# Delta layer: the filter table loaded in four parts around the rows, five buffers for the filter matrices, Gram copies in the room of the squares

## What is computed

```python
q = _short_conv(hidden_states @ Wq.T, conv_q)          # same for k and v; four taps, then silu
beta = jax.nn.sigmoid(hidden_states @ Wb.T)
delta_out = _delta_rule_chunkwise(q, k, v_direct, beta)
local_s = _fir(v_direct, fir_s)                        # 3, 15 and 63 taps, one filter per channel
local_m = _fir(v_direct, fir_m)
local_l = _fir(v_direct, fir_l)
o = probs[..., 0:1] * local_s + probs[..., 1:2] * local_m + probs[..., 2:3] * local_l \
    + probs[..., 3:4] * delta_out + probs[..., 4:5] * v_direct
```

## Time and profile before

| | |
|---|---|
| median of three runs | 4577.64 us |
| profiled execution | 4567.55 us |
| its span | 4565.8 us |
| busy: PE, DVE, ACT, POOL | 84%, 56%, 42%, 44% |

### The profile page before, as it was taken

The page is one execution under the profiler, slowest core; times in us unless marked ns, Lnnn a source line. Parts: engine busy times, 40 slices in busy tenths (PEclk is TensorE's granted clock), DMA queues, the critical chain, the costliest instruction groups (busy, mean ns, idle before and its releaser), DMA issues. The chain is left out here.

```text
span 4565.8 us, 70606 instructions
## 1 busy us (share of the span) xinstructions
PE 3829.3 (84%) x26088; PEld 2661.1 (58%) x26088; DVE 2545.7 (56%) x4540; ACT 1897.9 (42%) x3440; POOL 2020.5 (44%) x2061
## 2 busy tenths in 40 slices
PE   5677796799999519958999799788888888999995
PEld 2555774466767319943544455466666666656663
DVE  5566563455454582247777432498888887412223
ACT  3224132333333202225666412488888886112222
POOL 3531463323232216632332211298999998332223
PEclk8788897899999859978999999899999999999997
DMA  4774642200000529954544210111111111822224
GB/s 113 234 226 137 199 120 74 84 5 19 10 19 6 173 70 295 297 152 135 151 138 137 65 63 28 51 50 41 49 47 52 52 47 52 278 92 45 46 46 131
DMA packets 333687, 459.66 MB, mean 101 GB/s; under 512 B 70838, under 2 KB 245366, under 8 KB 329222
## 3 DMA queue, kind: packets, MB, share of 16 engines
q1 hardware_dynamic: 310710, 424.27, 30.5%
q0 software_dynamic: 22512, 30.36, 3.6%
q10 hardware_dynamic: 128, 0.52, 0.0%
HBM read 314.54 MB, written 140.51 MB: 100 GB/s over the span
## 5 line engine op out<-in xcount | busy, mean ns | idle before, releaser
L3565 POOL TENSOR_TENSOR mamba_hC<-mamba_h_t,mamba_cb 128x512 f32<-128x512 f32 x512 | 678.3, 1353 | 68.5 <-DVE mamba_h_t L3078 63.2
L3078 DVE TENSOR_TENSOR_SCAN mamba_h_t<-mamba_dA,mamba_pB 128x512 f32<-128x512 f32 x512 | 597.2, 1207 | 122.8 <-PE mamba_pB L3456 47.1
L3456 PE MATMUL mamba_pB<-ident,mamba_dBT 128*128 128x128 f32 x2048 | 328.8, 285 | 55.0 <-DVE mamba_h_t L3078 49.6
L3254 ACT ACTIVATE mamba_dA<-mamba_delta,mamba_a_neg 128x512 f32<-128x512 f32 x512 | 356.7, 713 | 21.5 <-DVE mamba_h_t L3078 20.9
L3456 PEld LDWEIGHTS mamba_pB<-ident,mamba_dBT 128*128 128x128 f32 x2048 | 240.4, 144 | 190.7 <-issue 99.0
L3465 PE MATMUL mamba_pY<-ident,mamba_hC 128*128 128x128 f32 x2048 | 321.3, 281 | 15.1 <-POOL mamba_hC L3565 14.1
L1911 POOL TENSOR_SCALAR mqa_prob<-mqa_prob,mqa_rinv 128x128 f32<-128x128 f32 (+3 forms) x256 | 136.7, 534 | 424.9 <-DVE mqa_rinv L1687 423.9
L2350 DVE TENSOR_REDUCE mha_nmax<-mha_pM 128x1 f32<-128x384 f32 (+3 forms) x352 | 215.9, 635 | 106.4 <-PE mha_pM L2658 103.2
L3245 ACT ACTIVATE mamba_dBT<-mamba_eT,mamba_b_t 128x512 f32<-128x512 f32 x384 | 273.8, 713 | 0.1
L1501 POOL DMA_INDIRECT top_sum<-top_y,top_xg x71 | 110.4, 1555 | 352.3 <-ACT top_y L1290 341.9
L3465 PEld LDWEIGHTS mamba_pY<-ident,mamba_hC 128*128 128x128 f32 x2048 | 248.1, 145 | 24.2 <-POOL mamba_hC L3565 23.5
(11 more groups left out here) (617 smaller groups left out, 8931.8 us busy)
## 6 DMA issues: line engine op xcount, KB each, us to landing
expert_w<-in_L_ffn_W SPq DMA_DIRECT2D x48, 1024.0 KB, 5.9
delta_shared<-delta_w SPq DMA_DIRECT2D x64, 576.0 KB, 4.9
mamba_cb<-mamba_c SPq DMA_DIRECT2D x128, 256.0 KB, 3.1
mha_qkT<-mha_parts_d SPq DMA_DIRECT2D x96, 256.0 KB, 5.1
delta_w<-delta_wst SPq DMA_DIRECT2D x32, 576.0 KB, 2.8
expert_w<-in_L_ffn_W SPq DMA_DIRECT2D x48, 256.0 KB, 6.4
top_w<-in_L_ffn_w SPq DMA_DIRECT2D x24, 512.0 KB, 10.7
top_slots<-top_y SPq DMA_DIRECT2D x1, 9159.0 KB, 36.5
```

The lines of the kernel that those rows point to most:

```text
L3078: nc.vector.tensor_tensor_scan(h_t[:, n % RH, :], dA[:, n % RA, :], pB[n % 2][:, :], 0.0, ALU.mult, ALU.add).then_inc(z["scan_ready"], 1)
L3254: nc.scalar.activation(dA[:, n % RA, :], delta[:, a % 2, ct, :], ACT.Exp, scale=a_neg[:, ct, s:s + 1])\
L3456: last = nc.tensor.transpose(pB[n % 2][:, tok(t)], dBT[:, r % RS, t, ct * P:(ct + 1) * P], c.ident[:, :])
L3565: nc.gpsimd.tensor_tensor(hC[:, n % RO, :], h_t[:, n % RH, :], cb[:, r % RC, :], ALU.mult)\
```

## The change

Five edits, all in `stage_delta`.

1. The table is loaded in four parts of 8 groups, sixteen transfers each (`load_table`): part 0 behind rows 1, part 1 behind rows 2, part 2 behind stores 0 to 3, part 3 behind rows 3, which now stand behind stores 4 to 7.
2. GpSimd has five buffers for filter matrices (`built_in`): the two of `wst` and three in `vn`, for matrices 0 to 24; the last seven use the two of `wst`. It builds matrices 0 to 2 in front of the deviation of rows 2 and 3 to 7 in front of that of rows 3.
3. 28 stores stand in front of the stores of V, the last four behind those of beta, in front of beta's load; none are left in the filter phase. The load of `vn` also waits for the stores out of it.
4. `gs` moves to `sq2`. VectorE's wait for the Gram stores moves from between its copies of K to the memset of the pads of `vp`, behind the gate copies.
5. V goes ahead of Gram copies 1 to 3, on TensorE, ScalarE and SyncE; V's load goes ahead of that of the Gram matrices.

```diff
+        spare = vn[:, :, :].rearrange("p a d -> p (a d)")[:, 0:3 * WCOLS].rearrange("p (n x) -> p n x", x=WCOLS)
+        built_in = [wst[:, 0, :], wst[:, 1, :], spare[:, 0, :], spare[:, 1, :], spare[:, 2, :]]
+        place = [g % 5 if g < 25 else (g - 25) % 2 for g in range(FG)]
+        turn_of = [place[:g].count(place[g]) for g in range(FG)]
...
-        gs = kr[:, NCH // 2:, :].rearrange("p n d -> p (n d)").rearrange("p (a t h i) -> p a t h i", a=NCH // 4, t=4, h=H)
+        gs = sq2[:, :, :, :].rearrange("p s k i -> p (s k i)").rearrange("p (a t h i) -> p a t h i", a=NCH // 4, t=4, h=H)
...
                 def store_table(g):
                     sp.wait_ge(z["w_built"], g + 1)
-                    sp.dma_start(w_d[g], wst[:, g % 2, :]).then_inc(w_st[g % 2], 16)
+                    sp.dma_start(w_d[g], built_in[place[g]]).then_inc(w_st[place[g]], 16)
+
+                def load_table(part):
+                    some = slice(part * FG // 4, (part + 1) * FG // 4)
+                    for r in range(R):
+                        sp.dma_start(table[C8 * r:C8 * (r + 1), some, :],
+                                     h_d.rearrange("(g c) x -> c g x", c=C8)[:, some, R - 1 - r:R - 1 - r + RUN])\
+                            .then_inc(table_in[part], 16)
...
@@ -4318,13 +4329,24 @@
                             sp.dma_start(h_d.rearrange("(k p) x -> p k x", p=P), hp).then_inc(z["h_st"], 16)
                             late_weights()
                             sp.wait_ge(z["h_st"], 16)
-                            for r in range(R):
-                                sp.dma_start(table[C8 * r:C8 * (r + 1), :, :],
-                                             h_d.rearrange("(g c) x -> c g x", c=C8)[:, :, R - 1 - r:R - 1 - r + RUN])\
-                                    .then_inc(z["table_in"], 16)
+                            load_table(0)
+                        if a == 2:
+                            load_table(1)
+                            for g in range(4):
+                                store_table(g)
+                            load_table(2)
+                            for g in range(4, 8):
+                                store_table(g)
+                        if a == 3:
+                            load_table(3)
                     if hf == 0:
-                        for g in range(3 * FG // 4):
+                        for g in range(8, FG - 4):
                             store_table(g)
+                    sp.wait_ge(z["vr_ready"], NCH // 2 * (hf + 1))
+                    for bb in range(HB):
+                        for i in range(CH // R):
+                            sp.dma_start(rows_of_runs(v_d, hf, bb, i, 0, NCH), vr[half_lanes(bb, i), :, :])\
+                                .then_inc(z["v_st"], 16)
                     for i in range(NCH // 4):
                         n = NCH // 4 * hf + i
                         sp.wait_ge(z["g_ready"], 2 * n + 2)
@@ -4332,11 +4354,13 @@
                             sp.dma_start(systems_by_row(g_d, hf, bb)[:, 4 * i * H:(4 * i + 4) * H, :],
                                          gs[lanes(bb), i, :, :, :].rearrange("p t h i -> p (t h) i"))\
                                 .then_inc(z["g_st"], 16)
-                    sp.wait_ge(z["vr_ready"], NCH // 2 * (hf + 1))
-                    for bb in range(HB):
-                        for i in range(CH // R):
-                            sp.dma_start(rows_of_runs(v_d, hf, bb, i, 0, NCH), vr[half_lanes(bb, i), :, :])\
-                                .then_inc(z["v_st"], 16)
+                    sp.wait_ge(z["v_st"], 16 * HB * CH // R * (hf + 1))
+                    if hf:
+                        sp.wait_ge(z["o_st"], 16 * hf)
+                    else:
+                        for i in range(2, 5):
+                            sp.wait_ge(w_st[i], 16 * place.count(i))
+                    sp.dma_start(vn[:, :, :], runs_of(v_d, hf)).then_inc(z["vn_in"], 16)
...
-                    sp.wait_ge(z["v_st"], 16 * HB * CH // R * (hf + 1))
-                    if hf:
-                        sp.wait_ge(z["o_st"], 16 * hf)
-                    sp.dma_start(vn[:, :, :], runs_of(v_d, hf)).then_inc(z["vn_in"], 16)
+                    if hf == 0:
+                        for g in range(FG - 4, FG):
+                            store_table(g)
...
                         if hf == 0:
-                            sp.wait_ge(w_st[g % 2], 16 * (g // 2 + 1))
+                            sp.wait_ge(w_st[place[g]], 16 * (turn_of[g] + 1))
                         if n >= 3:
                             sp.wait_ge(z["w_used"], n - 2)
                         sp.dma_start(wr[:, n % 3, :], w_d[g]).then_inc(w_ld[n % 3], 16)
-                        if hf == 0 and g < 4:
-                            store_table(3 * FG // 4 + 2 * g)
-                            store_table(3 * FG // 4 + 2 * g + 1)
...
                     dve.wait_ge(z["vr_ps"], NCH // 2 * (hf + 1))
                     nc.vector.memset(xt[:, :, :, :], 0.0)
-                    last = nc.vector.memset(vp[:, :, :, 0:PAD * HB], 0.0)
-                    last.then_inc(z["pads"], 1)
...
-                        if i == NCH // 4:
-                            dve.wait_ge(z["g_st"], 64 * NCH // 4 * (hf + 1))
                         nc.vector.tensor_copy(kr[:, 2 * i:2 * i + 2, :].rearrange("p n d -> p (n d)"), bank[6 + n % 2][:, :])\
                             .then_inc(z["kr_ready"], 1)
...
+                    dve.wait_ge(z["g_st"], 64 * NCH // 4 * (hf + 1))
+                    nc.vector.memset(vp[:, :, :, 0:PAD * HB], 0.0).then_inc(z["pads"], 1)
                     for q in range(SQ):
...
                     logits(base + HB - 1)
-                    if hf:
-                        act.wait_ge(z["kr_kept"], 32)
-                    for i in range(NCH // 4):
+                    def gram_copies(i):
                         n = NCH // 4 * hf + i
                         for odd in range(2):
                             act.wait_ge(z["g_ps"], 2 * n + odd + 1)
...
+                    gram_copies(0)
                     for i in range(NCH // 2):
                         n = NCH // 2 * hf + i
                         act.wait_ge(z["vr_ps"], n + 1)
@@ -4761,6 +4779,8 @@
                             act.wait_ge(z["v_kept"], 32)
                         nc.scalar.activation(vr[:, 2 * i:2 * i + 2, :].rearrange("p n d -> p (n d)"), bank[4 + n % 2][:, :],
                                              ACT.Copy).then_inc(z["vr_ready"], 1)
+                    for i in range(1, NCH // 4):
+                        gram_copies(i)
                     act.wait_ge(z["logit_ready"], base + HB)
                     nc.scalar.activation(by_chunk[BETA:BETA + H, :, :], by_chunk[BETA:BETA + H, :, :], ACT.Sigmoid)\
                         .then_inc(z["beta_ready"], 1)
...
-                    for i in range(NCH // 4):
+
+                    def gram(i):
                         n = NCH // 4 * hf + i
...
+                    gram(0)
                     pe.wait_ge(z["c_ready"], 3 * base + PAIRS)
                     pe.wait_ge(z["conv_done"], 3 * base + PAIRS)
                     for i in range(NCH // 2):
@@ -4959,6 +4981,8 @@
                                                            chunk(v_t, k, 2 * i + t), c.ident[:, :])
                         last.then_inc(z["vr_ps"], 1)
+                    for i in range(1, NCH // 4):
+                        gram(i)
                     pe.wait_ge(z["logit_ready"], base + HB)
                     for i in range(NCH // 2):
...
                 def matrix(g):
-                    if g >= 2:
-                        pool.wait_ge(w_st[g % 2], 16 * (g // 2))
+                    pool.wait_ge(table_in[4 * g // FG], 16 * R)
+                    if turn_of[g]:
+                        pool.wait_ge(w_st[place[g]], 16 * turn_of[g])
                     for f in "lms":
                         n = R * BLOCKS[f]
                         last = nc.gpsimd.tensor_tensor(
-                            wst[:, g % 2, WCOL[f]:WCOL[f] + n * C8].rearrange("p (x c) -> p x c", c=C8),
+                            built_in[place[g]][:, WCOL[f]:WCOL[f] + n * C8].rearrange("p (x c) -> p x c", c=C8),
                             table[:, g, FIRST[f]:FIRST[f] + n].unsqueeze(2).to_broadcast([P, n, C8]),
                             e8[:, :].unsqueeze(1).to_broadcast([P, n, C8]), ALU.mult)
                     last.then_inc(z["w_built"], 1)
@@ -5169,13 +5194,15 @@
                 for hf in range(HF):
                     for bb in range(HB):
                         variance(HB * hf + bb)
-                        if hf == 0 and bb == HB - 2:
+                        if hf == 0 and bb == 1:
                             pool.wait_ge(z["ones"], 1)
-                            pool.wait_ge(z["table_in"], 16 * R)
-                            for g in range(4):
+                            for g in range(3):
+                                matrix(g)
```

(4 more changed lines are left out.)

6 lines of the change are left out of this document (3 added, 3 removed).

## The result

The changed kernel took 4523.21 us, the median of five runs (4520.46 to 4544.29); the kernel before took 4574.22 in the same series (4567.22 to 4577.68, five runs). The ratio is 0.9902, its 95% interval 0.9877 to 0.9926. The profiled execution has a span of 4520.9 us against 4565.8.

What follows compares the result with a forecast made beforehand. Bound by SyncE's queue: table loads delay rows 2, later stores and loads delay beta and filter matrices. -32.0 + 16 + 4.1 - 14.7 + 1 = -25.6 us gives 4542 profiled, 4552 timed; range 4538 to 4567.

Steps and rivals of the forecast that it cites:

- A: First half's rows: rows 2, behind only a quarter of the table, start their statistics at 40.1 instead of 72.08, -32.0 us.
- S: First half's rows: rows 3, behind stores and table quarters, land by 75 us and cost +16, between 9 and 18.
- The other bound, 8 us: Table quarter on SyncE's queue: sixteen issues at 0.5 us each, 8 us, as the other end beside 10.9.
- The 5.5 us a quarter: Table load: a quarter's time if sixteen DMA engines served it, with rows 3 then late by about 9 us.
- B: From the rows' end to the first filter product: last stores and their buffer round trip delay beta, +4.1 us, 0 to +8.
- C: Filter phase, first half: no matrices left to build and store there, -14.7 us, ends -8 and -18.
- D: Second half: V's stores before the Gram stores, filter matrices 3 us later, mostly absorbed, +1 us, between -2 and +5.
- the carry: Whole time: the timed median's 10 us above the profiled execution carried over, 4542 to 4552; measurement can tell some 0.2%, 9 us.
- 3: Rows 3 hardly late: stores and quarters overlap on engines the table leaves idle, S = 3, 4539 us; chance 0.07.
- 2: Table load costs per load, not per packet: 2.14 us each, rows 3 land at 135, slower at 4614 us; chance 0.05.
- 1: Gain eaten in the middle: two landings of 14 us each before beta and filter matrices, 4575 us; chance 0.10.
- 4: Rows 2 stay late: GpSimd holds their deviation behind three matrices awaiting a late first quarter, 4556 us; chance 0.04.

Runs made afterwards that it cites:

- the second profile: The changed kernel itself, unedited, timed and profiled again in another series against the kernel before: 4533.59 us against 4571.0, ratio 0.9922.

## Why the prediction missed

**A, rows 2 earlier: right.** -32.0 predicted, -32.4 measured. But it was right for a reason that hid the mistake: VectorE itself isn't ready before 39.6 us, so a quarter of 5.6 us gives the same A as one of 8 to 10.9.

**S, rows 3 later than wanted: the step that failed.** 16 predicted, bounds 9 and 18; 4.6 measured (the rows' end moved by -27.8, A by -32.4), 4.0 in the second profile (-29.9 and -33.9). The wait is 5.32 us. Rows 3 were issued at 55.60 instead of the predicted 60.5 and landed 8.0 us later, at 63.6, instead of 75; VectorE wanted them at 58.3. The step said "all four quarters move the same packets as before, so I take a quarter of the table's time each", 43.5 / 4 = 10.9 us. The number of packets is the same, their speed is not: the earlier trace rows shows 80 GB/s at 0.59 of the engines, and I read that as the price of packets of this kind. It was the price of these packets in loads of 32 groups. In loads of 8 groups the engines give 136 GB/s at 0.54, and the quarters end in 5.6 to 7.4 us of queue. The experiments with whole, halved, quartered, eighth and lone loads show it: the speed follows the size of a load, the stretch of source plays no part, and a whole load is slow in its rear with no backlog too. By what mechanism stays open. The other bound, 8 us, was too high as well: it took 0.5 us an issue, near the Gram stores' 0.58, and the table's loads need 0.35 to 0.46.

The Trainium skill ("DMA: Bandwidth & Descriptors", section "Why a DMA increments its semaphore by 16 and not by 1") gave no more engines to the quarters than to the whole. The share didn't rise with the quarters, 0.54 against 0.59, which agrees with that. That the engines are eight it doesn't prove: 0.59 of sixteen is 9.4. The 5.5 us a quarter that I had tied to 16 engines came nearly true (5.55 to 7.41) without a larger share.

**B, from the rows' end to the first filter product: right.** +4.1 predicted, 61.3 - 56.6 = +4.7 measured (+6.7 in the second profile), by the steps named: GpSimd waits 28.86 us, the last stores hold the queue, beta's load right behind them. VectorE's new wait for the Gram stores is 5.97 us at 139.96 and costs nothing, since beta comes at 159.88.

**C, the filter phase: right.** -14.7 predicted; from the first product to the end of the last it is 252.58 - 162.28 = 90.3 us against 104.7, -14.4. The first two filter groups took 183.97 - 162.28 = 21.7 us instead of 37.9, as in the second half.

**D, the second half: right within its range.** +1 predicted; the marks moved by -37.5 and -37.8, so -0.3, with a spread of 3.6 between two profiles of one kernel.

**The sum and the carry.** With S at 4.6 instead of 16 the sum would have been -37.0 and the forecast 4540.6. The delta layer won 37.8. So S is 11.4 of the 28.8 us by which the forecast missed, and with S right the measured 4523.21 would still lie outside the range. Of the other 17.4 the other terms are 0.8, and 3.4 is the kernel before, which was 4574.22 in that series instead of 4577.64. The last 13 are in no term of the change. I put them down to the drawing of five runs, which is not shown for these runs one by one; what speaks for it is that the profiled one of them has the shortest stretch behind the change of all fourteen profiles, and that the second series, with a difference of 37.4, gives what the traces give. The step that failed here is the carry: I had counted on 0.2%, 9 us, as what a measurement can tell, while two medians of one kernel lie 10.4 us apart and the unchanged stretch varies by 25. The size of that part couldn't be foreseen, but the range had no room for it.

**The rivals.** 3 came nearest, rows 3 hardly late, S = 3 and 4539: its size of S was right, its reason, overlap of stores and quarters on engines that the table leaves idle, was a part at most, as the quarters alone are twice as fast. 2, cost per load, is what the eighths show: 0.36 us a load, not the 2.14 of the rival. The rule of the Trainium skill that I had put beside it ("DMA: Bandwidth & Descriptors", section "Bandwidth"), that transfers under 64 KB are dominated by their descriptors, did not bear on this step: loads of 43.5 KB are faster than those of 174 KB, and the measurement decides. At 22 KB the cost per load does take over. 1 (eaten in the middle) and 4 (rows 2 stay late) did not come: in B the first buffer came back at 151.80, 9.6 us after the last four stores began, and not 14, and rows 2 had no wait.

## What to carry to other kernels

A row of a slow transfer gives the price of that transfer, not of its packets: when a change cuts a load into parts, bound the part's price from below by the fastest packets of that kind that the trace shows anywhere, and by the issue time of a load, and not by division alone. If a long strided load keeps the DMA engines busy and moves few GB/s, as this one did, try it in smaller pieces and stop where the issuing queue becomes the limit. And mark a change at a place right behind it in the trace: the end of a 4.5 ms program moves by several us for reasons that have nothing to do with it.

## What the hardware showed that was not expected

A load of 8 partitions, 32 groups and 174 numbers, alone, is fast only in its first two thirds: it comes up to 155 GB/s and goes on at 53 and 46, at nearly the same share of the DMA engines. Queued behind one another, such loads moved 46 to 97 GB/s in the half-microseconds from 35 to 46 us. The same table took 34.24 us of queue in 16 loads (61 to 65 GB/s), 27.46 in 32 (75 to 88), 24.14 in 64 (113 to 136) and 46.12 in 128 (55, limited by issue at 0.36 us each). And the same instructions behind the change took 3344.7 and 3360.8 us in two profiles of one kernel.
